# Projecting k over its tokens in the interleaved order, in an attention and feed-forward kernel

## The reference

```python
qkv = encodings @ attn_w.T + attn_b
qkv = qkv.reshape(b, n, HEADS, 3 * HEAD).transpose(0, 2, 1, 3)
q, k, v = jnp.split(qkv, 3, axis=-1)
mask = jnp.arange(n)[:, None] <= jnp.arange(n)[None, :]
scores = jnp.einsum('bhki,bhqi->bhkq', k, q) / math.sqrt(HEAD)
scores = jnp.where(mask, scores, NEG_INF)
probs = jax.nn.softmax(scores, axis=2)
combined = jnp.einsum('bhkq,bhkl->bhql', probs, v)
out = combined.transpose(0, 2, 1, 3).reshape(b, n, HIDDEN) @ out_w.T + out_b
x = _layernorm(x + out)
...
acc = jax.lax.dot_general(q_lhs, q_rhs, ...)        # int8 x int8
x = _layernorm(x + acc.astype(jnp.float32) * lhs_scale * rhs_scale)
```

## Time and profile before

| | us |
|---|---|
| median of three runs | 279.83 |
| the profiled execution | 279.72 |
| its span on the core | 277.8 |
| TensorE busy | 245.3 (88%) |
| ScalarE busy | 198.6 (71%) |
| VectorE busy | 190.1 (68%) |
| GpSimd busy | 113.3 (41%) |
| TensorE's mean granted clock | 0.941 |

### The profile page before, as it was taken

The page is one execution under the profiler, slowest core; times in us unless marked ns, Lnnn a source line. Parts: engine busy times, 40 slices in busy tenths (PEclk is TensorE's granted clock), DMA queues, the critical chain, the costliest instruction groups (busy, mean ns, idle before and its releaser), DMA issues.

```text
span 277.8 us, 8316 instructions
## 1 busy us (share of the span) xinstructions
PE 245.3 (88%) x3084; PEld 171.1 (62%) x3084; DVE 190.1 (68%) x545; ACT 198.6 (71%) x448; POOL 113.3 (41%) x223
## 2 busy tenths in 40 slices
PE   8269746999999999999999999999999999999610
PEld 4137534777677777777777767676767677565300
DVE  4635954585969696969696969687878887723621
ACT  3893332667787978788887878787878777799541
POOL 7412140223335353535354545453636131523542
PEclk9658996999999999999999999999999999999965
DMA  4386358446835582578356744765465510110001
GB/s 132 131 210 112 86 120 244 90 162 110 209 72 171 90 233 57 165 126 216 72 177 116 205 83 153 138 191 99 154 118 177 93 40 6 40 40 4 19 19 38
DMA packets 50887, 32.77 MB, mean 118 GB/s; under 512 B 7200, under 2 KB 50848, under 8 KB 50848
## 3 DMA queue, kind: packets, MB, share of 16 engines
q1 hardware_dynamic: 50704, 32.06, 47.1%
q10 hardware_dynamic: 144, 0.20, 0.3%
HBM read 17.17 MB, written 14.68 MB: 115 GB/s over the span
## 4 chain that ended last, share of the span: by engine, by line
PE 80%; DMA 5%; SPq 3%; DVE 3%; POOL 3%; ACT 3%; issue 2%; ACTq 0%; POOLq 0%; DVEq 0%
PE pv_bank L905 18%; PE dve_bank L868 17%; PE act_bank L868 13%; PE act_bank L926 6%; PE act_bank L871 5%; PE dve_bank L871 5%; DMA k_stat<-imagek 3%; PE act_bank L936 3%; PE dve_bank L950 3%; PE dve_bank L968 3%; DMA imagek<-qk_parts 2%; PE pv_bank L1005 2%; PE act_bank L959 1%; PE dve_bank L916 1%; SPq L341 1%
## 5 line engine op out<-in xcount | busy, mean ns | idle before, releaser
L672 DVE TRANSPOSE_TENSOR_REDUCE part_max<-dve_bank 128x16 f32<-128x512 f32 (+1 forms) x192 | 116.2, 616 | 44.0 <-PE dve_bank L871 41.9
L476 ACT ACTIVATE probs<-act_bank 128x512 f32<-128x512 f32 (+1 forms) x192 | 101.1, 530 | 38.5 <-PE act_bank L871 37.0
L868 PE MATMUL dve_bank<-q_move,k_stat 124*128 124x128 bf16 (+3 forms) x512 | 71.7, 243 | 6.3 <-DMA k_stat<-imagek 5.4
L868 PE MATMUL act_bank<-q_move,k_stat 128*128 128x128 bf16 (+3 forms) x512 | 67.7, 235 | 2.8 <-issue 2.8
L868 PEld LDWEIGHTS dve_bank<-q_move,k_stat 124*128 124x128 bf16 x512 | 40.3, 118 | 34.7 <-DVE part_max L672 7.6
L905 PE MATMUL pv_bank<-probs,v_stat 128*32 128x256 f32 (+3 forms) x1024 | 61.1, 311 | 0.0
L411 POOL TENSOR_TENSOR qk_rest<-qk_f,qk_parts 128x512 f32<-128x512 f32 x15 | 17.4, 1158 | 83.3 <-ACT qk_f L494 83.3
L871 PE MATMUL dve_bank<-causal,identb 128*128 128x128 bf16 (+1 forms) x192 | 46.8, 244 | 0.0
L868 PEld LDWEIGHTS act_bank<-q_move,k_stat 128*128 128x128 bf16 x512 | 41.9, 114 | 7.3 <-issue 4.9
L871 PE MATMUL act_bank<-causal,identb 128*128 128x128 bf16 (+1 forms) x192 | 45.8, 239 | 0.0
L905 PEld LDWEIGHTS pv_bank<-probs,v_stat 128*32 128x32 f32 x1024 | 20.3, 108 | 19.4 <-issue 9.8
(11 more groups left out here) (91 smaller groups left out, 316.1 us busy)
## 6 DMA issues: line engine op xcount, KB each, us to landing
imageq<-qk_parts SPq DMA_DIRECT2D x32, 192.0 KB, 2.0
imagek<-qk_parts SPq DMA_DIRECT2D x32, 192.0 KB, 2.1
q_move<-imageq SPq DMA_DIRECT2D x32, 192.0 KB, 3.9
k_stat<-imagek SPq DMA_DIRECT2D x32, 192.0 KB, 4.2
xt_in<-xt_dram SPq DMA_DIRECT2D x16, 128.0 KB, 4.6
x_in<-x_dram SPq DMA_DIRECT2D x16, 128.0 KB, 2.4
out_dram<-o SPq DMA_DIRECT2D x16, 128.0 KB, 2.0
q_move<-shift SPq DMA_DIRECT2D x32, 8.0 KB
```

Source lines behind the costliest of these rows:

```text
L476: act.activation(probs[u][:, 0:cols], act_bank[at % ACT_BANKS][:, 0:cols], ACT.Exp, scale=SCALE).then_inc(act_emptied, 1)
L672: dve.tensor_reduce(o32, dve_bank[at % DVE_BANKS][:, 0:n * (TOK - key)].rearrange("k (c q) -> k c q", q=32), op=ALU.max, axis=AX.X, apply_ ...
L868: pe.matmul(tiles[:, j, :], keys, q_move[b % QK_RING][0:rows, p0 + j, key:TOK], start=(j == 0), stop=False, skip_group_check=True)
```

## The change

The moving operand of k's projection is read in the interleaved order, `"c (b k) -> c k b"`: for each of 64 places four tokens that lie 64 float32 apart. The product so stands in PSUM in the order in which the parts want it. The five instructions that empty k's bank (L493 and L494 for w = 1, L577, L829, L831) now read and write 256 elements side by side. q is unchanged. On each engine the same instructions stand in the same order with the same waits; the shapes of these alone differ.

```diff
--- before.py
+++ after.py
@@ -486,12 +486,8 @@
                     wait_ring(act, image_written, b - 2, 4, 4)
                 act.wait_ge(act_filled, at + 1)
                 src = act_bank[at % ACT_BANKS][:, 0:TOK]
-                first, whole = part[b % 2][0][:, w, :], qk_f[:, w, :]
-                if w == 1:
-                    src = src.rearrange("c (b k) -> c b k", b=4)
-                    first, whole = (d.rearrange("c (k b) -> c b k", b=4) for d in (first, whole))
-                act.activation(first, src, ACT.Identity, bias=bias[:, w:w + 1])
-                act.activation(whole, src, ACT.Identity, bias=bias[:, w:w + 1]).then_inc(act_emptied, 1)
+                act.activation(part[b % 2][0][:, w, :], src, ACT.Identity, bias=bias[:, w:w + 1])
+                act.activation(qk_f[:, w, :], src, ACT.Identity, bias=bias[:, w:w + 1]).then_inc(act_emptied, 1)
 
             def v_from_psum(b):
 
@@ -573,8 +569,8 @@
                 act.activation(first_again[0][:, 0, :], q, ACT.Identity, bias=bias[:, 0:1]).then_inc(act_emptied, 1)
                 at = ACT_AT["k", 0]
                 wait(act, qk_split, 0, 1)
-                k = act_bank[at % ACT_BANKS][:, 0:TOK].rearrange("c (b k) -> c b k", b=4)
-                act.activation(first_again[0][:, 1, :].rearrange("c (k b) -> c b k", b=4), k, ACT.Identity,
+                k = act_bank[at % ACT_BANKS][:, 0:TOK]
+                act.activation(first_again[0][:, 1, :], k, ACT.Identity,
                                bias=bias[:, 1:2]).then_inc(act_emptied, 1)
                 zeros(q_move[1][:, :, :].rearrange("r p q -> r (p q)").bitcast(F32), 1024).then_inc(act_setup, 1)
 
@@ -823,9 +819,9 @@
                 at = ACT_AT["k", 0]
                 dve.wait_ge(bias_in, 16)
                 dve.wait_ge(act_filled, at + 1)
-                k = act_bank[at % ACT_BANKS][:, 0:TOK].rearrange("c (b k) -> c b k", b=4)
-                k_first = part[0][0][:, 1, :].rearrange("c (k b) -> c b k", b=4)
-                k_rest = qk_rest[:, 1, :].rearrange("c (k b) -> c b k", b=4)
+                k = act_bank[at % ACT_BANKS][:, 0:TOK]
+                k_first = part[0][0][:, 1, :]
+                k_rest = qk_rest[:, 1, :]
                 dve.tensor_scalar(k_first, k, bias[:, 1:2], None, ALU.add).then_inc(first_read, 1)
                 dve.wait_ge(first_read, 2)
                 dve.scalar_tensor_tensor(out=k_rest, in0=k, scalar=bias[:, 1:2], in1=k_first, op0=ALU.add,
@@ -923,7 +919,10 @@
                 if w == 0:
                     wait_ring(pe, xt_loaded, b, 1)
                 bank = act_ring(("qk"[w], b))
-                pe.matmul(bank[:, 0:TOK], wqkv[:, w, :], xt_in[b % XT_RING][:, :],
+                tokens = xt_in[b % XT_RING][:, :]
+                if w == 1:
+                    tokens = tokens.rearrange("c (b k) -> c k b", b=4)
+                pe.matmul(bank[:, 0:TOK], wqkv[:, w, :], tokens,
                           start=True, stop=True).then_inc(act_filled, 1)
 
             def project_v(b):
```

## The result

The changed kernel takes 285.36 us (median of four runs, 284.91 to 286.00), the kernel before 280.0 beside it (279.44 to 281.36): 1.0177 times as long, with a 95% interval of 1.0149 to 1.0204. The forecast was 284.2 us, with 278.5 to 285.3 as its range and 283.6 to 285.3 for the likeliest case. The profiled execution (284.91) lies within both, and so does the ratio put on the 279.83 us of before (284.8); the median of the four runs is 0.06 us above.

The account below looks back on a forecast made before the run. The prediction took TensorE's streaming to bound the steady part and DMAs, behind ScalarE's and VectorE's reads of k, the start. On 279.72 us it summed -1.08 + 0.43 + 5.12 = +4.47 to 284.2 us, range 278.5 to 285.3.

Parts of the forecast that it names:

- the likeliest case: k's projections, 256-byte step: TensorE's streaming time doubles, 0.43 us more each, 284.2 us in all; chance 0.56.
- TensorE has no slack from 50 us on: Steady part, 50 to 215 us: TensorE streams 164.96 of 165.00 us; longer streaming moves the end, shorter ScalarE gives nothing.
- A float32 column with a step of 256 bytes costs twice: k's projection on TensorE: 0.833 ns a column doubles, 0.43 us more a projection; bounds 0 and 0.51 us.
- 12 projections pay in full, batches 0 and 1 nothing: k's projections: batches 4 to 15 pay 12 x 0.427 = 5.12 us; batches 0 and 1, behind the warm-up, pay nothing.
- The start gains 1.08 us and gives back 0.43: Start: faster k reads save 0.65 us in batch 0 and 0.43 in batch 2, whose projection costs 0.43.
- the image goes out about 0.65 us earlier: Batch 0: VectorE's L829 and L831 each fall to about 0.42 us, so SyncE issues the image 0.65 us sooner.
- The clock takes up to 0.3 us: Half-clock stretch 44.09 to 47.30 us: half of the 0.65 us lead is lost if the clock rises when it did.
- ScalarE's busy time falls by 9.5 us: ScalarE's two writes of k, 15 batches: 15 x (0.84 + 0.73 - 0.94) = 9.5 us less busy time.
- The free step: Rival, k's projection: the step costs TensorE nothing, only the start's gain remains, 278.6 us; chance 0.27.
- the small cost: Rival, k's projection: the step costs 16%, 0.07 us a projection, 279.5 us, no change; chance 0.05.
- The cost above a doubling: Rival, k's projection: the step costs more than a doubling, 0.76 us a projection, 288.5 us; chance 0.08.
- The evacuation isn't relieved: Rival, emptying k's bank: something else slows the writes, start gains nothing, 285.3 us with the doubling; chance 0.04.

Follow-up runs that it names:

- the run with the evacuation alone: Kernel before with only the five reads of k made side by side, projection unchanged, k's order wrong; ratio 0.9975.
- step2: Changed kernel with k's tokens read with a step of 2 float32 (8 bytes) in place of 64, k's order wrong; ratio to the kernel before 0.9993.
- the run with the projection alone: Kernel before with only k's projection reading tokens with the 256-byte step, old scattered writes kept; 286.17 us, ratio 1.0218.
- with the clock held: 20 warm-up matmuls added before batch 2's scores; ratio to the kernel before 0.9952 on that kernel, 1.0113 on the changed one.
- the fastest kernel: Kernel before, k untouched, with GpSimd's memset of k_stat[1] after VectorE's copy to bfloat16 and 20 warm-up matmuls; 276.71 us, ratio 0.9897.

## Why the prediction was right, step by step

*TensorE has no slack from 50 us on.* Right: the period went up by all that the projection did, 0.44 of 0.43 us, and a ScalarE with less to do changed nothing in the run with the evacuation alone.

*A float32 column with a step of 256 bytes costs twice.* Right: 0.43 us a projection was forecast and 0.43 measured. L680 on VectorE, with the same pattern, was the row to go by. That its cost carries over as a doubling (0.43 us) and not as its own 1.00 ns an element (0.51) was a choice that no row supported, and it was lucky that it came out to the hundredth. The weight load of L868 has 8 bytes, and by step2 that is on the other side of the edge. The forecast had taken it for a small case of the same thing, but 8 and 16 bytes are far apart: 0.02 and 0.45 us.

*12 projections pay in full, batches 0 and 1 nothing.* Right for the 12: from batch 4's start to the end of the span the changed kernel takes 233.3 us and the one before 227.9, 5.4 more for a forecast of 5.12. Of batches 0 and 1 nothing can be seen either: in the run with the projection alone their four matmuls hold the chain for 1.72 us, before for 1.80.

*The start gains 1.08 us and gives back 0.43.* The step that failed is its first half, "the image goes out about 0.65 us earlier": measured 0.05 us (SyncE's first issue at 8.76 against 8.81), and the first scores at 18.08 and not at 17.35. The copy L686, which the working used as a fixed 0.57 us, was stretched by a memset on GpSimd, and the sign stood in the rows: 0.57 for this one, where the same copy took 0.43 in the batches after it. The other half, 0.43 us of ScalarE's reads against 0.43 of the projection, came out as worked out once the clock was held. The wait for batch 2's keys ended at 43.27, near the 43.4 of the forecast, and that is luck: in this execution the clock's earlier first rise brought the lead, and with the clock held there is none.

*The clock takes up to 0.3 us.* Too small: it took the whole lead of 0.82 us in the profiled execution, after it had brought most of it. The sum was +4.47 for +5.19 us between the profiled executions. Up to batch 4 it had -0.65 for a measured +0.03, from there on 5.12 for 5.37, and 0.2 us went outside the span. With the clock held the start gives 0.00, so the term of 0.65, without which the sum is 284.8, is the one that was missing.

*ScalarE's busy time falls by 9.5 us.* It fell by 4.6. The forecast added up durations of operations that overlap: k's two start 0.57 us apart, and the next operation starts before they end.

*The rivals.* The free step fell by the kernel with the projection alone; the small cost too. The cost above a doubling didn't show. *The evacuation isn't relieved* was wrong in its mechanism, since ScalarE's writes came down to 0.47 us as forecast, but what it says of the start, that it gains nothing, is what happened, and its 285.3 us are nearer to the measured 284.8 to 285.4 than the 284.2.

**What stays open.** What decides when the clock rises behind batch 2's scores (at 47.1 us before, at 48.5 in the changed kernel, during 49 to 50 with the projection alone) isn't shown, and each kernel has one trace. Nor is it shown whether the missing gap before the first scores makes the clock rise earlier in the fastest kernel, or whether that execution only fell that way.

## What to carry to other kernels

A rearrangement isn't free wherever it is put: ask which of the two engines has slack, and give it to that one. Here it cost 0.3 us of ScalarE's busy time a batch (4.9 us over the kernel), which gave nothing back in the full part, against 0.43 of TensorE's, all of which was paid. If an engine has to read with a step, count how many elements it takes out of each 16 bytes; two were enough and one cost a doubling. And when an operation takes longer than its twin of the same shape elsewhere in the trace, find out why before using it as a term, since a gain ahead of it may only make it longer.

## What the runs showed of the hardware

- TensorE's moving operand in float32, 256 columns twice: 0.63 us side by side, 0.65 with a step of 8 bytes, 0.64 in pairs with jumps of 256 bytes, 1.08 with a step of 16 bytes, 1.06 with 256.
- Float32 weights with a step of 8 bytes, 64 columns: 16 matmuls with their loads in 0.64 us instead of 0.61 to 0.62.
- ScalarE, 256 elements out of PSUM: 0.47 us written side by side; with a step of 4 elements 0.84 (bfloat16) and 0.73 (float32).
- VectorE's copy from float32 to bfloat16 (512 elements) and its float32 product with a scalar (128 elements) don't run beside GpSimd's memset of 2048 float32: 0.43 became 1.60, and 0.28 became 1.36, each ending 0.1 to 0.3 us after the memset. Two others weren't held up: L831, with PSUM as an input, took 0.68 us wholly within the memset (before) and 0.68 where none ran (the fastest kernel), and L829, the difference of two tensors in SBUF, took 0.41 within it (changed kernel) and 0.41 with the memset moved away. The Trainium skill (SBUF — State Buffer, Who interferes with whom) names a pair of ports that VectorE's copies share with GpSimd; the runs agree with it.
- The granted clock fell from 1.00 to 0.50 during 40 to 41 us in the kernel before, after TensorE had idled from 36.2 to 39.1, and stayed there until 47.1. With 20 matmuls without a use in these gaps it stayed at 1.00, and the stretch from batch 2's scores to batch 4 took 4.36 us instead of 5.79.
